# Clearing the slot regions' tails from two queues, moving the last values from SP, and forming shares and slots later, in a mixture-of-experts phase

## The reference

```python
logits = xf @ router_w.T + experts_bias
rw, sel = jax.lax.top_k(logits, K)            # K = 2 of E = 8 experts
rw = jax.nn.softmax(rw, axis=-1)              # the shares
cw = (jax.nn.one_hot(sel, E) * rw[..., None]).sum(axis=1)
g, u = einsum('td,edh->teh', xf, w1), einsum('td,edh->teh', xf, w3)
moe_out = einsum('te,teh,ehd->td', cw, silu(g) * u, w2)
...
k = _split_heads(key @ Wk.T + bk)
v = _split_heads(value @ Wv.T + bv)
```

## Time and profile before

| | |
|---|---|
| median of 3 runs | 1101.4 us |
| profiled execution | 1100.62 us, of which the span 1098.8 us |
| PE busy | 902.1 us (82%) |
| DVE busy | 734.4 us (67%) |
| ACT busy | 534.6 us (49%) |
| POOL busy | 505.7 us (46%) |
| mean granted PE clock | 0.915 |

### The profile page before, as it was taken

The page is one execution under the profiler, slowest core; times in us unless marked ns, Lnnn a source line. Parts: engine busy times, 40 slices in busy tenths (PEclk is TensorE's granted clock), DMA queues, the critical chain, the costliest instruction groups (busy, mean ns, idle before and its releaser), DMA issues. The chain is left out here.

```text
span 1098.8 us, 24814 instructions
## 1 busy us (share of the span) xinstructions
PE 902.1 (82%) x9121; PEld 644.6 (59%) x9121; DVE 734.4 (67%) x2271; ACT 534.6 (49%) x848; POOL 505.7 (46%) x566
## 2 busy tenths in 40 slices
PE   5820988875887776699999915899999999899997
PEld 1210666653555554466666613788888888666665
DVE  6753588887776766287887746777777775255553
ACT  2423676753433333276666632556656665232321
POOL 4300146656777677055555556765665630011110
PEclk9965999996888897799999968999999999899999
DMA  8524444425123223524333221121111310123431
GB/s 246 211 66 128 111 145 133 139 62 193 46 71 81 68 71 95 152 87 125 117 121 123 95 79 37 40 55 42 54 50 41 100 50 12 49 60 101 116 78 38
DMA packets 84742, 101.35 MB, mean 92 GB/s; under 512 B 36144, under 2 KB 57456, under 8 KB 83856
## 3 DMA queue, kind: packets, MB, share of 16 engines
q1 hardware_dynamic: 55088, 77.88, 23.3%
q0 software_dynamic: 8192, 16.79, 5.3%
q10 hardware_dynamic: 21344, 5.12, 2.7%
HBM read 64.88 MB, written 30.67 MB: 87 GB/s over the span
## 5 line engine op out<-in xcount | busy, mean ns | idle before, releaser
L1006 POOL TENSOR_TENSOR moe_h_lo<-moe_hid,moe_h_hi 128x512 f16<-128x512 f32 x78 | 90.6, 1162 | 103.6 <-ACT moe_h_hi L1159 98.6
L1685 ACT ACTIVATE split_table<-attn_psT 128x1024 f32<-128x1024 f32 x64 | 65.6, 1025 | 100.2 <-PE attn_psT L1564 100.2
L1153 ACT ACTIVATE moe_act_g<-moe_psG,split_unscale 128x512 f32<-128x512 f32 x110 | 75.5, 687 | 71.1 <-PE moe_psU L1088 40.0
L1263 DVE SCALAR_TENSOR_TENSOR moe_hid<-moe_psU,split_to_hidden,moe_act_g 128x512 f32<-128x512 f32 x110 | 80.9, 747 | 38.9 <-ACT moe_act_g L1153 38.8
L1748 DVE TENSOR_REDUCE split_table<-attn_psN 128x16 f32<-128x1024 f32 x62 | 75.5, 1218 | 12.3 <-PE attn_psN L1539 12.0
L1159 ACT ACTIVATE moe_h_hi<-moe_hid 128x512 f16<-128x512 f32 x110 | 68.3, 621 | 31.5 <-DVE moe_hid L1263 28.7
L1000 POOL DMA_INDIRECT scratch_xs<-cell_xn,res_row x64 | 62.4, 976 | 29.1 <-issue 18.2
L1000 POOL DMA_INDIRECT scratch_xs<-moe_xn,res_row x64 | 62.3, 973 | 24.2 <-issue 18.7
L285 POOL TENSOR_SCALAR ffn_shifted<-ffn_mv 128x4 f32<-128x4 f32 x16 | 3.7, 229 | 148.4 <-DVE ffn_mv L266 117.7
L1481 POOL DMA_INDIRECT cell_h<-scratch_ys,res_slot x64 | 62.2, 972 | 20.8 <-issue 20.8
L1576 PE MATMUL attn_psO<-heads_vheads,split_table 128*64 128x18 f32 x2048 | 71.3, 212 | 0.1
(11 more groups left out here) (277 smaller groups left out, 2660.2 us busy)
## 6 DMA issues: line engine op xcount, KB each, us to landing
mlstm_vals<-in_values SPq DMA_DIRECT2D x16, 544.0 KB, 3.7
mlstm_keys<-in_keys SPq DMA_DIRECT2D x16, 512.0 KB, 3.6
scratch_ys<-cell_h SPq DMA_DIRECT2D x26, 256.0 KB, 2.0
res_x<-in_x SPq DMA_DIRECT2D x16, 256.0 KB, 6.1
early_ctxT<-in_ctxT SPq DMA_DIRECT2D x16, 256.0 KB, 6.4
attn_in_ctxT<-attn_in_ctxT ACTq DMA_DIRECT2D x64, 64.0 KB
scratch_x<-split_table SPq DMA_DIRECT2D x16, 256.0 KB, 2.3
out<-raw_keys SPq DMA_DIRECT2D x32, 128.0 KB, 2.3
```

Of the source, the lines that this page charges most:

```text
L1006: pool.tensor_tensor(h_lo[u % 3][c][:, :], hid[u % 2][c][:, :], h_hi[u % 3][c][:, :], ALU.subtract).then_inc(lo_done[c], 1)
L1153: act.activation(act_g[c][:, :], psG[c][:, :], ACT.Silu, scale=sw.unscale[:, 0:1]).then_inc(silu_done, 1)
L1263: v.scalar_tensor_tensor(out=hid[u % 2][c][:, :], in0=psU[c][:, :], scalar=sw.to_hidden[:, 0:1], in1=act_g[c][:, :], op0=ALU.mult, op1=ALU ...
L1685: act.activation(probT[i % 2][:, :, :, :, :].rearrange("p r b m q -> p (r b m q)"), psT[:, :], ACT.Exp).then_inc(prob_done, 1)
```

## The change

- Four of the eight clears go to ACT's queue: in the last four rounds ACT does k_out(g), v_out(g), and then reads a region's end and issues the clear (regions 4 to 7). SP issues the other four.
- The moves of the values of groups 12 to 15 (16 DMAs, in four steps, each waiting for the step before to land) leave ACT and go to SP, after the first five loads of slot tiles and before the sixth.
- The slot of every token is formed by DVE at the end of unit 20 instead of in `map_tiles` (`find_slots`).
- The tanh on ACT and the shares on DVE go to the end of the phase.

```diff
+        def clear_tail(eng, e):
+            tail = eng.value_load(tails[0:1, e:e + 1], min_val=0, max_val=E0 * REGION - GROUP)
+            eng.dma_start(s["xs"][bass.ds(tail, GROUP), :].rearrange("(p t) d -> p t d", p=P), y[0][:, :, :]).then_inc(tails_in, 16)
+
+        def move_values(eng, g):
+            staged, final = (...)
+            eng.wait_ge(v_raw, ONE + g + 1)
+            eng.wait_ge(v_moved, ONE + 16 * 4 * g)
+            for b2 in range(2):
+                for half in range(2):
+                    eng.dma_start(final[...], staged[...]).then_inc(v_moved, 16)
...
-            for e in range(E0):
-                tail = sp.value_load(...)
-                sp.dma_start(...)
+            for e in range(E0 // 2):
+                clear_tail(sp, e)
...
             for j in range(NB - 1):
                 load(j)
+            for g in range(GROUPS - AHEAD, GROUPS):
+                move_values(sp, g)
...
             v_out(GROUPS - 1 - AHEAD)
+            move_values(act, GROUPS - 1 - AHEAD)
             high_part(GROUPS - 1, 1)
+            act.wait_ge(blank_done, ONE + 1)
             for g in range(GROUPS - AHEAD, GROUPS):
                 k_out(g)
                 v_out(g)
-            act.wait_ge(gap_done, ONE + GROUPS)
-            act.activation(tanh[:, :], gap[:, :], ACT.Tanh, scale=0.5).then_inc(tanh_done, 1)
+                act.wait_ge(tails_done, ONE + 1)
+                clear_tail(act, g - GROUPS + E0)
             xT_out(GROUPS)
...
             high_part(UNITS - 1, 1)
+            act.wait_ge(gap_done, ONE + GROUPS)
+            act.activation(tanh[:, :], gap[:, :], ACT.Tanh, scale=0.5).then_inc(tanh_done, 1)
...
-            shares()
             v.wait_ge(map_done, ONE + 1)
...
                     weights_of(u + 2 - GROUPS)
+                if u == GROUPS + AHEAD:
+                    find_slots()
             y_out_(UNITS - 2)
             y_out_(UNITS - 1)
+            shares()
```

More of the change, by code:

```diff
@@ L952, in group @@
             return slice(g * TILES, (g + 1) * TILES)
+        def clear_tail(eng, e):
+            tail = eng.value_load(tails[0:1, e:e + 1], min_val=0, max_val=E0 * REGION - GROUP)
+            eng.dma_start(s["xs"][bass.ds(tail, GROUP), :].rearrange("(p t) d -> p t d", p=P), y[0][:, :, :]).then_inc(tails_in, 16)
+        def move_values(eng, g):
+            staged, final = (given.ctxT[:, n * GROUP:(n + 1) * GROUP].rearrange("p (t n c) -> p t n c", t=TILES, n=2) for n in (g + 1, g))
+            eng.wait_ge(v_raw, ONE + g + 1)
+            eng.wait_ge(v_moved, ONE + 16 * 4 * g)
+            for b2 in range(2):
+                for half in range(2):
+                    eng.dma_start(final[half * S:(half + 1) * S, :, b2, :], staged[b2 * S:(b2 + 1) * S, :, half, :]).then_inc(v_moved, 16)
         @block.sync
@@ L962, in _ @@
             sp.wait_ge(tails_done, ONE + 1)
-            for e in range(E0):
-                tail = sp.value_load(tails[0:1, e:e + 1], min_val=0, max_val=E0 * REGION - GROUP)
-                sp.dma_start(s["xs"][bass.ds(tail, GROUP), :].rearrange("(p t) d -> p t d", p=P), y[0][:, :, :]).then_inc(tails_in, 16)
+            for e in range(E0 // 2):
+                clear_tail(sp, e)
             sp.wait_ge(map_done, ONE + 1)
@@ L1165, in v_out @@
             def v_out(g):
-                staged, final = (given.ctxT[:, n * GROUP:(n + 1) * GROUP].rearrange("p (t n c) -> p t n c", t=TILES, n=2) for n in (g + 1, g))
                 act.wait_ge(v_full, ONE + g + 1)
                 act.activation(given.ctxT[:, (g + 1) * GROUP:(g + 2) * GROUP], psKV[:, :], ACT.Copy).then_inc(v_raw, 1)
[L1169 to L1173, removed]
             xT_out(0)
@@ L1181, in _ @@
                     v_out(u - 1 - AHEAD)
+                    move_values(act, u - 1 - AHEAD)
                 gate(u, 0)
@@ L1308, in map_tiles, with find_slots @@
                 v.tensor_scalar(rows[:, :], first_row[:, :], float(E0 * REGION), None, ALU.min).then_inc(map_done, 1)
+            def find_slots():
                 step(v.tensor_tensor(shift[:, :], ends[:, :], tiles[:, :], ALU.subtract))
```

## The result

The changed kernel took 1106.98 us (median of 11 runs), the kernel before 1102.51 us beside it: a ratio of 1.0043, 95% interval 1.0028 to 1.0058. It is slower by some 4.7 us; I had forecast 1.35 us, which a measurement can't tell from none.

The account below looks back on a forecast made before the run. PE was taken to bound the slot tiles, ACT's queue of moves the start of up(16). The terms -0.4 + 1.4 + 0.35 gave +1.35 us, a forecast of 1102.7 us, with a range from 1099.4 to 1107.0.

Parts of the forecast that it names:

- Bound and place: Slot tiles are bound by PE; only what makes PE late at their head or holds it inside adds time.
- Terms 1 to 3: Last value rounds, last clear, first slot tile: up(16) starts at 460.55 against 460.95 us, a gain of 0.4.
- that case: Last value rounds: if the clock returns at the same moment as before, v_out(15) ends at 450.8 us.
- The reading that the last clear replaces the moves on the path: Ahead of up(16): ACT's moves leave the path and the last clear, behind v_out(15), takes their place; gain 0.4 us.
- Term 4: End of unit 20: DVE's `find_slots` delays turn(23) and up(22), costing 1.4 us.
- Term 5: At turn(21): SP's value moves hold back load(5), so PE waits 0.35 us.
- the sign of being wrong: At turn(21): a PE wait of over 2 us in the profile would show the prediction wrong.
- The rival of late moves: At turn(21): moves of 5.0 us or more on SP; at 6.3 PE waits 4.9, total +5.9 us; chance 0.19.
- The clock's case: Last value rounds: clock doesn't fall or returns at once, up(16) 3.3 us earlier, total -2.6 us; chance 0.13.

Follow-up runs that it names:

- e1: Changed kernel with SP issuing the four value moves one behind each of its first four stores, not ahead of the sixth load; ratio to the kernel before 0.9999.
- e7: Changed kernel with only two of the four value moves ahead of the sixth load, the others behind SP's first two stores; ratio to the kernel before 0.9994.
- e4: Changed kernel with ACT's four clears issued two by two behind v_out(12) and v_out(13); ratio to the kernel before 0.9935.
- e6: Changed kernel with ACT's clears early, slots formed behind the table of tiles, and moves behind SP's first four stores; ratio to the kernel before 0.9932.
- e3: Changed kernel with all eight clears on SP again; ratio to the kernel before 0.9939.
- e13: Changed kernel unedited, run once more for a second profile; one run without a ratio, 210.5 us from `tails` to the first gather.
- e9: Changed kernel with 48 unused matmuls on PE ahead of turn(16) and 12 behind it; ratio to the kernel before 1.0057.

## Why the prediction was wrong

- Bound and place: right. What changed in the stage lies in PE's waits at the three places named (the head, turn(21), turn(23)) and in how fast PE worked behind the first two, and nowhere else on the path.
- Terms 1 to 3, the head: the sum was right (-0.4 forecast, -0.25 measured) by errors that cancel, which is luck. v_out(15) ended 17.4 us behind `tails` and not 15.7. Of the 1.7, 0.9 is the clock, which was no sooner back than before: 16.6, the prediction's own figure for that case, is what e1, e7, e4 and e6 show. The other 0.8 is v(12), at the low clock here as in seven other profiles (2.08 us, and 1.16 in the kernel before), which no edit explains. Against that the register load was hidden, where I had put 0.9, the last clear and the read of the first row together took 2.8 for 3.3, and load(0) to up(16) took 6.2 for 6.45. The reading that the last clear replaces the moves on the path was right, and e3 and e4 show what it cost: 6.4 us of head in both, once the 0.7 of v(12) is taken off e4.
- Term 4, `find_slots`: right, 1.54 for 1.4.
- Term 5, the moves on SP, is the step that failed: "PE waits 0.35" at turn(21) was 3.01 and, in e13, 2.25, over the 2 us that the prediction itself named as the sign of being wrong. The term is the difference of two times of 24 us. load(5) went out 22.8 us after load(0) and not 21.6 (22.0 in e13): the first move took the 5.0 forecast, the second 5.4 for 4.2, as its four issues took 3.81 us, and the third 4.1. The tile landed 0.2 later still. And PE was ready 22.7 after load(0) and not 23.95, mostly since I took the 17.5 us from up(16) to turn(21) from a profile with a slow start that lasted longer. All three errors point one way: 0.35 + 1.2 + 0.2 + 1.3 = 3.0. The forecast stood 0.35 us beyond a threshold, and each microsecond there counts in full; only the last of the three gives something back, as PE came to turn(21) 1.05 us sooner after up(16).
- Missing in the sum: the clock that such a wait takes down, 1.46 and 1.7 us. Term 5 with it came to 3.01 + 1.46 - 1.05 = 3.4 us where 0.35 stood, and that is nearly all of the forecast's error.
- The rival of late moves had the right place and sign, and its own threshold of 4.3 us a move was passed (4.98, 5.39 and 4.14; in e13 4.93, 4.68 and 4.14). Its price was added up wrongly: with 6.3 us for each move the terms give a landing at 4.8 + 21.5 + 0.8 + 2.7 = 29.8 and a wait of 5.9, not 28.2 and 4.9, and so +6.9 in all; no run came near 6.3.
- The clock's case did not come. From k(13) on a projection took 2.07 us until v(14), as before, and v(12), ahead of the rounds, ran at the low clock as well.

## What to carry to other kernels

Where a term is the difference of two long paths that meet at a buffer, forecast the margin with the errors of both, and add what the idle time does to the matrix engine's clock. When work is taken off one queue, look for what stands last on the queue that gets it: a clear that all loads wait for belongs ahead of the rounds, and transfers that nobody awaits belong behind the loads that somebody does.

## What was not expected of the hardware

- Waits of PE of 3.0 and 2.25 us in the full slot stage were followed by matmuls at 1.2 GHz (granted clock 0.72 from 481 to 487 us, and 0.80 from 483 to 490 in e13) and 1.5 and 1.7 us more of work; waits of 0.63 to 1.65 us in four other profiles, and one of 2.21 in e9, were not. The Trainium skill ("TensorE: Matmul & The Clock Gate", section "Part 1: The HAM clock gate (the "warmup" mystery)") has it that the clock follows how busy the engine has lately been; that agrees in kind, and these rows give no sure length of wait at which it is lost.
- A register load on ACT behind an ACTIVATE of 0.60 us took no time of its own (the clear went out 0.07 us after it), while one clear followed another on SP after 1.1 to 1.4 us (1.4 before, 1.2 in the changed kernel, 1.1 in e3).
- The attention phase's first stretch, with the same work, took 77.1 to 82.1 us over the profiles: more than the whole effect that was looked for. The granted clock goes with it: over the whole piece it was 0.76 to 0.78 in the six profiles of 77.1 to 77.3 us, and 0.66 to 0.71 in the six of 79.1 to 82.1.
- The same holds in small for one projection: v(12) took 1.16 or 2.08 us, by the clock, in kernels that don't differ there.
